# Seven block products in both stages of an AdaLN and low-rank FFN kernel

## The chip, the cores and the metric

The kernel runs on one core of one Trainium2 chip. The metric is the device time of one execution in microseconds, the median of several runs. PE is the matrix engine (TensorE), PEld its weight loads, ACT ScalarE, DVE VectorE, POOL GpSimd and SP the engine that issues the DMAs. Each engine takes its instructions in order and waits on semaphores.

## The reference, cut to what matters

`x` is 16 batches of 512 tokens by 1024 channels. Everything is float32.

```python
q_emb = relu(cond @ W3 + b3)                        # (16, 1024)
y = relu(((n * x + sum_over_tokens(x)) * q_emb[:, None, :]) @ W2 + b2)   # n = 512
base = y @ W_base + b_base                          # 1024 x 1024
shared = (y @ A_s) @ B_s                            # rank 16
gates = softmax(y @ W_router + b_router)            # 6 experts, the top 2 are kept
routed = sum over e of ((y @ A_r[e]) * w[e]) @ B_r[e]   # rank 16 each
out = x + base + shared + routed
```

The three factors `W_router`, `A_r` and `A_s` stand side by side in `acat` (1024 x 118), the `B` factors in `bcat` (118 x 1024).

## The kernel before

Activations lie transposed, channels on the 128 partitions and the 512 tokens of a batch along the free axis, so that a tile is 128 x 512. Every float32 product is three matmuls (`three`, L856 to L860): operands are split into a rounded high part (fp32r, made by ACT) and the low remainder (made by DVE, or by POOL for weights), and hi x hi, hi x lo and lo x hi are added up in PSUM.

**First stage** (W2), unrolled over eight pairs of batches. The 2 x 2 blocks are the two halves of the channels and the two batches of a pair: G11, G21 are batch 0, G12, G22 batch 1. Seven products of blocks replace eight (`NPROD`), in `product` (L902): four groups j of output tiles, each with four k, 16 threes in all. ACT loads and sums the x tiles (`source`, L495), waits for POOL's `shift_of` (L416), scales them, and makes the high parts (`high`, L516). DVE makes the low parts (`low`, L663) and the block sums (`t1` to `t4`). Partial results go from PSUM to the buffers `pbuf` and `ubuf` and are added there (`copy_p0`, `make_w`, `make_u`, L527 and L689); two sets of four banks alternate (`SETB`). Results go through `yring` and are stored in DRAM without the relu. Between these, SP and POOL split W_base into high and low, one 128 x 512 chunk at a time, two per pair (`load_wbase`, `save_wbase`, `split`).

**Second stage** (W_base), a loop of one batch (`batch`, L942) on each engine. y is loaded again (`load_y`), relu and the splits are made (`y_high`, `y_low`), and each of eight output tiles takes eight threes with W_base: 64 threes per batch. Beside them stand the eight threes of the projection on `acat` into bank 6, four small transposes of the router's rows (L959), the gate work on DVE (`gate`, L800, eleven small steps each waiting for the one before), four transposes of the gates (L967), the product with the gates, and eight threes of the low-rank factors (`low_rank`). `evac_out` (L789) adds bias and residual, and SP stores.

The order of work on each engine is written out by hand; nothing else plans it. SP holds all DMAs in one order, and a wait in it holds back all that follow. ACT's order in a pair, with the calls put on fewer lines:

```python
def pair(i, last=False):          # ACT, L549
    high(i, 1); source(i, G12); copy_p0(i)
    high(i, 2); source(i, G22); c11(i)
    high(i, 3); high(i, 4); high(i, 5)
    ...                           # next_first, high(i, 6), next_rest
```

Of the kernel before, what the change touches and what calls it, by code (L numbers as in the profile page):

```python
# [5 lines left out]
F32 = mybir.dt.float32  # L6
# [5 lines left out]
P = 128  # L12
PAIR = 2
# [13 lines left out]
H = 4  # L27
G11, G22, G12, G21 = range(4)
HELD_IN = [G11, G21, G12, G12, G11, G22, G21]
SETB = [0, 0, 1, 0, 1, 0, 1]  # L30
CONTINUES = (1, 6)
BATCH_OF = {G11: 0, G21: 0, G12: 1, G22: 1}
HALF_OF = {G11: 0, G21: 1, G12: 0, G22: 1}
SOURCE_NO = {G11: 0, G21: 1, G12: 2, G22: 3}


def adaln_ffn(nc, xT, condT, w3, b3, w2, b2, wbase, bbase, acat, bcat, brouter, outT, E, R):
# [6 lines left out]
    NCH = wbase.shape[0]  # L44
    CW = wbase.shape[2]
    HALF = K // 2
    WARM = 8
    OPS = NPROD * H

    y_dram = nc.dram_tensor("y_scratch", (NB, K, P, T), F32, kind="Internal").ap()  # L50
    wbh_dram = nc.dram_tensor("wb_hi_scratch", (NCH, P, CW), F32, kind="Internal").ap()
    wbl_dram = nc.dram_tensor("wb_lo_scratch", (NCH, P, CW), F32, kind="Internal").ap()

    with ExitStack() as ctx:
# [41 lines left out]
        sb("early_pad2", [P, NPROD * H, T], F32, early)  # L96
        sb("early_pad3", [P, 4 * H, T], F32, early)
# [5 lines left out]
        phase1 = ExitStack()  # L103
        w2_hi = sb("w2_hi", [P, NPROD, H, T], F32R, phase1)
        w2_lo = sb("w2_lo", [P, NPROD, H, T], F32R, phase1)
        phase1.close()

        wb_hi = sb("wb_hi", [P, 2, K, CW], F32R)  # L110
        a_hi = sb("a_hi", [P, K, AC], F32R)
        a_lo = sb("a_lo", [P, K, AC], F32R)
        sb("pad4", [P, H * T - 2 * K * AC])
        a_sb = sb("a_sb", [AC, T])
        hw = sb("hw", [AC, T])
        hw_hi = sb("hw_hi", [AC, T], F32R)
        hw_lo = sb("hw_lo", [AC, T], F32R)
        sb("pad5", [P, 4, T])
        wb_lo = sb("wb_lo", [P, 2, K, CW], F32R)
        low_hi = sb("low_hi", [AC, D], F32R)  # L120
        low_lo = sb("low_lo", [AC, D], F32R)
        wtok = sb("wtok", [P, TT, E])
        logits = sb("logits", [P, TT, E])
        lmax = sb("lmax", [P, TT])
        shifted = sb("shifted", [P, TT, E])
        ex = sb("ex", [P, TT, E])
        den = sb("den", [P, TT])
        rden = sb("rden", [P, TT])
        gates = sb("gates", [P, TT, E])
        beats = sb("beats", [P, TT, E, E])  # L130
        ties = sb("ties", [P, TT, E, E])
        rank = sb("rank", [P, TT, E])

        STAGE_AT = [H * G11 + k for k in range(H)] + [H * G22 + k for k in range(H)]
        RES_AT = [H * G12 + k for k in range(H)] + [H * G21 + k for k in range(H)]
# [3 lines left out]
        A_BANK, GATE_BANK = 6, 7  # L139
        Q_BANK, QT_BANK = 4, 6  # L140
        q_tok = [ps[:, QT_BANK + h, 0:HALF * NB].rearrange("p (m b) -> p m b", b=NB) for h in range(2)]
        tok = ps[:, GATE_BANK, 0:TT * E].rearrange("p (t c) -> p t c", t=TT)
# [71 lines left out]
        def slot(i, n, k):  # L214
            return H * ((i + n) % 2) + k
# [809 lines left out]
```

## Time and profile before

| | us |
|---|---|
| Median of 3 runs | 1557.67 (1557.47 to 1558.39) |
| Profiled execution | 1559.65 |
| Its span | 1557.8 |
| First stage, first matmul to last | 18.1 to 653.9 |
| Second stage | 658.1 to 1554.5 |
| PE / DVE / ACT / POOL busy | 1524.4 / 627.9 / 458.5 / 101.6 |

Matmuls are pipelined: a matmul lasts about 0.39 us, but the next one starts 0.23 us after it, so rows of single matmuls have to be read by their starts. A group's "idle before" counts only what remains after this overlap. Times in the rows are microseconds from the start of the span.

### The profile page before, as it was taken

The numbers are of one execution on the slowest core, as the hardware profiler recorded it, in microseconds if no ns is written. First come the engines' busy times: TensorE is split into PE (matmuls) and PEld (weight loads), VectorE is DVE, ScalarE is ACT, GpSimd is POOL, SyncE is SP. The second block draws the span as 40 slices with busy tenths as digits, with TensorE's granted clock in tenths as the row PEclk, the third lists the DMA queues.
The fourth block names the chain that finished last, engine by engine and source line by source line (L and its number), as shares of the span: only waits on it lengthen the run. The fifth ranks groups of instructions, "written<-read, shape, count | busy, mean of one in ns | idle before, by whom it ended". The sixth has DMA issues, their size and how long they took to land.

```text
span 1557.8 us, 18539 instructions
## 1 busy us (share of the span) xinstructions
PE 1524.4 (98%) x6688; PEld 1239.5 (80%) x6688; DVE 627.9 (40%) x1064; ACT 458.5 (29%) x869; POOL 101.6 (7%) x117
## 2 busy tenths in 40 slices
PE   6889999999999999899999999999999999999999
PEld 3668888888888888788888888888888888888887
DVE  3676555555646465612322321331232232233122
ACT  5646465555556564101101110110110110111010
POOL 2841000000000001000000000000000000000000
PEclk8899999999999999999999999999999999999999
DMA  7043425243434257434233323413413432341321
GB/s 277 28 155 116 165 105 169 98 160 108 149 108 166 92 179 275 161 112 162 75 117 131 119 83 121 162 40 121 162 65 114 145 107 95 121 161 41 121 108 54
DMA packets 107781, 196.67 MB, mean 126 GB/s; under 512 B 12258, under 2 KB 12258, under 8 KB 107736
## 3 DMA queue, kind: packets, MB, share of 16 engines
q1 hardware_dynamic: 107736, 196.10, 35.7%
q8 instruction: 25, 0.41, 0.1%
q14 instruction: 20, 0.16, 0.0%
HBM read 120.55 MB, written 75.50 MB: 126 GB/s over the span
## 4 chain that ended last, share of the span: by engine, by line
PE 95%; DVE 2%; ACT 1%; issue 1%; POOL 0%; DMA 0%; SPq 0%; DVEq 0%; POOLq 0%
PE ps L858 31%; PE ps L859 31%; PE ps L860 31%; DVE src L672 1%; DVE act_lo L667 1%; ACT src L505 0%; PE ps L967 0%; PE ps L959 0%; DMA src<-in_xT 0%; POOL w_lo L425 0%; ACT act_hi L524 0%; ACT w_hi L493 0%; DVE ubuf L693 0%; DVE w_lo L754 0%; ACT src L499 0%
## 5 line engine op out<-in xcount | busy, mean ns | idle before, releaser
L858 PE MATMUL ps<-act_hi,wb_hi 128*128 128x512 f32 x1024 | 404.1, 395 | 4.2 <-issue 4.2
L860 PE MATMUL ps<-act_hi,wb_lo 128*128 128x512 f32 x1024 | 400.5, 391 | 0.0
L859 PE MATMUL ps<-act_lo,wb_hi 128*128 128x512 f32 x1024 | 400.5, 391 | 0.0
L858 PE MATMUL ps<-act_hi,w_hi 128*128 128x512 f32 x896 | 351.0, 392 | 20.8 <-ACT pbuf L532 15.7
L859 PE MATMUL ps<-act_lo,w_hi 128*128 128x512 f32 x896 | 349.8, 390 | 0.0
L860 PE MATMUL ps<-act_hi,w_lo 128*128 128x512 f32 x896 | 349.8, 390 | 0.0
L858 PEld LDWEIGHTS ps<-act_hi,wb_hi 128*128 128x128 f32 x1024 | 192.7, 188 | 46.4 <-issue 4.6
L860 PEld LDWEIGHTS ps<-act_hi,wb_lo 128*128 128x128 f32 x1024 | 192.8, 188 | 41.9
L859 PEld LDWEIGHTS ps<-act_lo,wb_hi 128*128 128x128 f32 x1024 | 192.9, 188 | 40.4
L667 DVE TENSOR_TENSOR act_lo<-src,act_hi 128x512 fp32r<-128x512 f32 x224 | 158.6, 752 | 151.7 <-ACT act_hi L524 151.7
L858 PEld LDWEIGHTS ps<-act_hi,w_hi 128*128 128x128 f32 x896 | 169.1, 189 | 58.9 <-ACT pbuf L532 15.8
L859 PEld LDWEIGHTS ps<-act_lo,w_hi 128*128 128x128 f32 x896 | 169.2, 189 | 35.0
L860 PEld LDWEIGHTS ps<-act_hi,w_lo 128*128 128x128 f32 x896 | 168.9, 188 | 35.3
L524 ACT ACTIVATE act_hi<-src 128x512 fp32r<-128x512 f32 x220 | 132.4, 628 | 203.7 <-PE ps L860 187.9
L629 ACT ACTIVATE act_hi<-src 128x512 fp32r<-128x512 f32 x128 | 80.9, 632 | 237.4 <-PE ps L860 237.2
L811 DVE TENSOR_TENSOR logits<-ps,br_sb 128x24 f32<-128x24 f32 x16 | 2.9, 182 | 364.0 <-PE ps L959 364.0
L785 DVE SCALAR_TENSOR_TENSOR act_lo<-src,act_hi 128x512 fp32r<-128x512 f32 x128 | 88.4, 693 | 95.9 <-ACT act_hi L629 95.9
L795 DVE SCALAR_TENSOR_TENSOR src<-ps,bb_sb,src 128x512 f32<-128x512 f32 x128 | 87.6, 745 | 77.9 <-PE ps L860 77.9
L672 DVE TENSOR_TENSOR src<-src 128x512 f32<-128x512 f32 x128 | 91.1, 772 | 63.5 <-ACT src L505 63.5
L505 ACT ACTIVATE src<-src,shift,qn 128x512 f32<-128x512 f32 x124 | 91.0, 805 | 18.0 <-POOL shift L419 18.0
L633 ACT ACTIVATE a_sb<-ps 118x512 f32<-118x512 f32 x16 | 9.6, 597 | 283.8 <-PE ps L860 283.8
L499 ACT ACTIVATE src<-src 128x512 f32<-128x512 f32 x124 | 76.3, 617 | 16.7 <-DMA src<-in_xT 16.6
(84 smaller groups left out, 899.9 us busy)
## 6 DMA issues: line engine op xcount, KB each, us to landing
src<-in_xT SPq DMA_DIRECT2D x256, 256.0 KB, 3.9
y_scratch<-yring SPq DMA_DIRECT2D x128, 256.0 KB, 2.5
src<-y_scratch SPq DMA_DIRECT2D x128, 256.0 KB, 5.3
outT<-src SPq DMA_DIRECT2D x128, 256.0 KB, 2.1
r<-in_w SPq DMA_DIRECT2D x16, 256.0 KB, 7.8
wraw<-in_wbase SPq DMA_DIRECT2D x16, 256.0 KB, 3.3
wb_hi_scratch<-wst_hi SPq DMA_DIRECT2D x16, 256.0 KB, 2.0
wb_lo_scratch<-wst_lo SPq DMA_DIRECT2D x16, 256.0 KB, 2.5
```

What stands on the lines that cost most here:

```text
L499: nc.scalar.activation(src[:, t, :], src[:, t, :], ACT.Copy, accum_out=vsum[:, t:t + 1]).then_inc(x_summed, 1)
L505: nc.scalar.activation(src[:, t, :], src[:, t, :], ACT.Identity, bias=shift[:, t:t + 1], scale=qn[:, H * HALF_OF[g] + k, 2 * i + BATCH_OF[ ...
L524: nc.scalar.activation(act_hi[:, slot(i, n, k), :], src[:, H * HELD_IN[n] + k, :], ACT.Copy).then_inc(hi_done, 1)
L629: nc.scalar.activation(act_hi[:, k, :], src[:, STAGE_AT[k], :], ACT.Relu).then_inc(y_hi_done, 1)
L633: nc.scalar.activation(a_sb[:], ps[0:AC, A_BANK, :], ACT.Copy).then_inc(a_copied, 1)
L667: nc.vector.tensor_tensor(act_lo[:, s, :], src[:, H * HELD_IN[n] + k, :], act_hi[:, s, :].bitcast(F32), ALU.subtract).then_inc(lo_done, 1)
L672: nc.vector.tensor_tensor(src[:, H * out + k, :], src[:, H * a + k, :], src[:, H * b + k, :], ALU.subtract).then_inc(t_ready, 1)
L785: nc.vector.scalar_tensor_tensor(act_lo[:, k, :], src[:, STAGE_AT[k], :], 0.0, act_hi[:, k, :].bitcast(F32), ALU.max, ALU.subtract).then_i ...
L795: nc.vector.scalar_tensor_tensor(r, ps[:, bank, :], bb_sb[:, m:m + 1], r, ALU.add, ALU.add).then_inc(out_evac, 1)
L858: nc.tensor.matmul(out, w_hi, a_h, start=start, stop=False, skip_group_check=onto)
L859: nc.tensor.matmul(out, w_hi, a_l, start=False, stop=False, skip_group_check=onto)
L860: return nc.tensor.matmul(out, w_lo, a_h, start=False, stop=stop, skip_group_check=onto)
```

## The change

Both stages take pairs of batches and seven block products. The products 2, 3, 4 and 6 are added in PSUM onto what the banks hold (`ONTO`), so that banks 0 to 3 carry all the sums; product 1 goes to banks 4 and 5 and is added by DVE. Before a bank is accumulated further, ACT copies it (`copy_p0`, `copy_u2`, `copy_u4`) to `buf1` to `buf3`, in which the results are finished.

In the first stage the projections on `acat` (`project_y`, a `three` after a group of products 4, 5, 6 and of the next pair's 0), the transposes and the gate work are put between the products. For them y is split again (`y_high`, `y_low`); `y_low` writes over the buffer that was stored. The gated rows go to DRAM (`hw_dram`). The second stage only has the seven products, the low-rank threes and the residual; its low-rank input for product 6 is the difference of two batches.

W_base's seven block sums are made in the first stage in 60 pieces of at most 128 x 256 (`piece` on SP and on POOL), 4 in pair 0 and 10 or 9 in each of pairs 1 to 6, one set of buffers for all. Both stages are unrolled on all engines. The diff, cut to its core (`...` marks what is left out):

```diff
+ONTO = (2, 3, 4, 6)
+PIECES = [(k, c, n) for k in range(H) for c in range(2) for n in (3, 2, 4, 5, 0, 1, 6)]
+PIECES += [(None, c, None) for c in range(D // PW)]
...
+        @block.sync
+            def piece(step):
+                if step > 0:
...
+                    sp.wait_ge(prep_made, step)
...
+                        sp.dma_start(wbh_dram[n, :, k, cols], wh[:].bitcast(F32)).then_inc(prep_saved, 16)
+                        sp.dma_start(wbl_dram[n, :, k, cols], wl[:].bitcast(F32)).then_inc(prep_saved, 16)
+                    sp.wait_ge(prep_saved, 32 * step)
+                if step < len(PIECES):
...
+                    elif n == 3:
+                        raw(ws, Q21)
+                        raw(wt, Q22)
...
+            def pair(i):
+                todo = list(POINTS.get(i, range(0)))
...
+                point(9)
+                point(8)
...
+                for j in range(H):
+                    sp.wait_ge(relu_done, four(i, j))
+                    sp.dma_start(y_dram[2 * i, j], buf1[:, j, :]).then_inc(buf1_stored[j], 16)
+                point(7)
...
+                for k in range(H):
+                    sp.wait_ge(lo_done, op_no(i, 4, k))
+                    load_next(i, G22, k)
+                point(5)
...
+                point(4)
+                for k in range(H):
+                    sp.wait_ge(lo_done, op_no(i, 5, k))
+                    load_next(i, G11, k)
+                point(3)
+                if last:
+                    load_weights(4)
+                for j in range(H):
+                    sp.wait_ge(c12_done, four(i, j))
+                    sp.dma_start(y_dram[2 * i + 1, j], buf1[:, j, :]).then_inc(buf1_stored[j], 16)
+                point(2)
+                for k in range(H):
+                    sp.wait_ge(lo_done, op_no(i, 6, k))
+                    load_next(i, G21, k)
+                point(1)
+                if last:
+                    load_weights(5)
+                for j in range(H):
+                    sp.wait_ge(c22_done, four(i, j))
+                    sp.dma_start(y_dram[2 * i + 1, H + j], buf3[:, j, :]).then_inc(buf3_stored[j], 16)
+                point(0)
...
+        @block.gpsimd
+            for i in range(1, LAST):
+                todo = list(POINTS[i])
+                for q, more in ((G12, 6), (G22, 4), (G11, 2), (G21, 0)):
+                    while len(todo) > more:
+                        piece(todo.pop(0))
+                    shift_of(i + 1, q)
...
+        @block.scalar
+            def pair(i):
+                last = i == LAST
+                if i > 0:
+                    x_scale(i, G21)
+                    for j in range(H):
+                        high(i, 1, j)
+                        y_high(i - 1, C21, j)
+                        if j == 0:
+                            copy_h(i - 1, GB)
+                        else:
+                            copy_p0(i, j - 1)
+                    copy_p0(i, H - 1)
+                for j in range(H):
+                    high(i, 2, j)
+                    if j == 0 and i > 0:
+                        exponent(i - 1, GB)
+                    if j > 0:
+                        relu(i, j - 1)
...
+                for j in range(H):
+                    high(i, 4, j)
+                    if j > 0:
+                        copy_u4(i, j - 1)
+                    if j == 2 and i > 0:
+                        exponent(i - 1, GA)
+                    if j >= 2:
+                        y_high(i, C11, j - 2)
+                    if not last:
+                        x_sum(i + 1, G12, j)
+                copy_u4(i, H - 1)
+                if not last:
+                    x_scale(i + 1, G12)
+                for j in range(H):
+                    high(i, 5, j)
+                    if j > 0:
+                        c12(i, j - 1)
+                    if j in (1, 2):
+                        y_high(i, C11, j + 1)
+                    if not last:
+                        x_sum(i + 1, G22, j)
+                c12(i, H - 1)
+                if not last:
+                    x_scale(i + 1, G22)
+                for j in range(H):
+                    high(i, 6, j)
+                    y_high(i, C12, j)
+                    if not last:
+                        x_sum(i + 1, G11, j)
...
+        @block.vector
+            def y_low(i, c, j):
+                if c == C11:
+                    dve.wait_ge(buf1_stored[j], 16 * (2 * i + 1))
...
+            def pair(i):
+                if i > 0:
+                    c21(i - 1, H - 1)
+                    for j in range(H):
+                        low(i, 1, j)
+                        y_low(i - 1, C21, j)
+                        t2(i, j)
+                    gate_logits(i - 1, GB)
+                    gate_weights(i - 1, GB)
+                for j in range(H):
+                    low(i, 2, j)
+                    if j > 0:
+                        c11(i, j - 1)
...
+                for j in range(H):
+                    low(i, 4, j)
+                    if j == 1 and i > 0:
+                        gate_logits(i - 1, GA)
...
+                if i > 0:
+                    gate_weights(i - 1, GA)
...
+                for j in range(H):
+                    low(i, 6, j)
+                    if j > 0:
+                        c22(i, j - 1)
+                    y_low(i, C12, j)
...
+        @block.tensor
+            def pair(i):
+                for j in range(H):
+                    group(i, 0, j)
+                    if i > 0:
+                        project_y(i - 1, C21, j)
+                        if j == 1:
+                            turn_h(i - 1, GB)
+                    elif j == 0:
+                        turn(1)
...
+                for j in range(H):
+                    group(i, 1, j)
+                    if j == 2 and i > 0:
+                        turn_gates(i - 1, GB)
+                for j in range(H):
+                    group(i, 2, j)
+                if i > 0:
+                    turn_h(i - 1, GA)
+                for j in range(H):
+                    group(i, 3, j)
+                if i > 0:
+                    turn_gates(i - 1, GA)
+                for j in range(H):
+                    group(i, 4, j)
+                    project_y(i, C11, j)
+                for j in range(H):
+                    group(i, 5, j)
+                    project_y(i, C12, j)
+                for j in range(H):
+                    group(i, 6, j)
+                    project_y(i, C22, j)
```

In `group`, product 1 waits for `c11_done` of group j - 2 before it takes a Z bank again; `c12` on ACT waits for `project_y` to have read C11 from the same buffer; `y_high` uses two tiles in turn and waits for the `project_y` two before.

## Rows read from the trace of the kernel before

**Rows 1.** The page, parts 1 and 2: busy us; tenths of the granted clock in 40 slices.

```profile
PE 1524.4 (98%) x6688; PEld 1239.5 (80%) x6688; DVE 627.9 (40%) x1064; ACT 458.5 (29%) x869; POOL 101.6 (7%) x117
...
PEclk8899999999999999999999999999999999999999
```

**Rows 2.** The page, part 4: the chain that ended last, by engine.

```profile
PE 95%; DVE 2%; ACT 1%; issue 1%; POOL 0%; DMA 0%; SPq 0%; DVEq 0%; POOLq 0%
```

**Rows 3.** Groups by line, forms apart: first matmul of each three.

```profile
L858 PE MATMUL ps<-act_hi,wb_hi 128*128 128x512 f32 x1024 | 404.1, 395 | 4.2 <-issue 4.2
...
L858 PE MATMUL ps<-act_hi,w_hi 128*128 128x512 f32 x896 | 351.0, 392 | 20.8 <-ACT pbuf L532 15.7 <-issue 2.7 <-DVE act_lo L667 2.4
...
L858 PE MATMUL ps<-act_hi,a_hi 128*118 128x512 f32 x128 | 50.4, 394 | 0.0
...
L858 PE MATMUL ps<-hw_hi,low_hi 118*128 118x512 f32 x128 | 50.2, 392 | 0.0
```

**Rows 4.** One pair by windows; then PE timeline: gate transposes of batches 0, 1.

```profile
120.60:196.80 76.20, 76.20 (x338) 63.06 (x336) 44.06 (x70) 43.82 (x87) 4.50 (x8) 1.00 0.43 149
...
694.56 0.60 PE L967 MATMUL ps<-ident,wrow 128*118 128x128 f32 x4
...
750.39 0.60 PE L967 MATMUL ps<-ident,wrow 128*118 128x128 f32 x4
```

**Rows 5.** PE timeline: start, us, instruction, idle; the three long idle times.

```profile
29.28 0.42 PE L875 MATMUL ps<-ident,qrow 16*128 16x16 f32 x4
45.41 0.80 PE L858 MATMUL ps<-act_hi,w_hi 128*128 128x512 f32 x1 [15.71 <-ACT pbuf L532]
...
105.36 0.39 PE L860 MATMUL ps<-act_hi,w_lo 128*128 128x512 f32 x1
108.22 0.76 PE L858 MATMUL ps<-act_hi,w_hi 128*128 128x512 f32 x1 [2.47 <-issue]
...
653.53 0.39 PE L860 MATMUL ps<-act_hi,w_lo 128*128 128x512 f32 x1
658.11 0.77 PE L858 MATMUL ps<-act_hi,wb_hi 128*128 128x512 f32 x1 [4.19 <-issue]
```

**Rows 6.** PE timeline behind the second of them.

```profile
109.64 0.63 PE L858 MATMUL ps<-act_hi,w_hi 128*128 128x512 f32 x1
110.07 0.63 PE L859 MATMUL ps<-act_lo,w_hi 128*128 128x512 f32 x1
```

**Rows 7.** ACT and DVE timeline in pair 1: scales, a copy, splits.

```profile
213.32 2.94 ACT L505 ACTIVATE src<-src,shift,qn 128x512 f32<-128x512 f32 x4 [0.31 <-POOL shift L419]
...
218.76 0.69 ACT L539 ACTIVATE yring<-ps,b_sb 128x512 f32<-128x512 f32 x1 [0.79 <-PE ps L860]
219.34 2.19 ACT L524 ACTIVATE act_hi<-src 128x512 fp32r<-128x512 f32 x4
...
220.00 2.50 DVE L667 TENSOR_TENSOR act_lo<-src,act_hi 128x512 fp32r<-128x512 f32 x4 [1.22 <-ACT act_hi L524]
```

**Rows 8.** Timeline of one gate: exponent, and the last step.

```profile
741.49 0.22 ACT L635 ACTIVATE ex<-shifted 128x24 f32<-128x24 f32 x1 [7.19 <-DVE shifted L814]
...
744.31 0.36 DVE L833 COPY wrow<-wtok 128x384 f32<-128x384 f32 x1
```

**Rows 9.** SP timeline; page part 6; L267 and L282 after 575 us: landings.

```profile
588.56 0.44 SPq L271 DMA_DIRECT2D wraw<-in_wbase  x1
593.92 0.32 SPq L275 DMA_DIRECT2D wb_hi_scratch<-wst_hi  x1
...
wb_lo_scratch<-wst_lo SPq DMA_DIRECT2D x16, 256.0 KB, 2.5
...
DMA to landing us min/median/max: 2.0/2.1/8.8
...
DMA to landing us min/median/max: 5.8/8.5/12.5
```

**Rows 10.** DVE and POOL timeline in pair 0, both busy.

```profile
70.69 6.88 DVE L672 TENSOR_TENSOR src<-src 128x512 f32<-128x512 f32 x4
...
66.78 6.84 POOL L430 TENSOR_TENSOR r<-r,s 128x512 f32<-128x512 f32 x4
```

**Rows 11.** The last matmul; the span ends at 1557.8.

```profile
1554.13 0.39 PE L860 MATMUL ps<-hw_hi,low_lo 118*128 118x512 f32 x1
```

More of the change, by code:

```diff
@@ L28 @@
 G11, G22, G12, G21 = range(4)
[L29 to L31 removed]
+ONTO = (2, 3, 4, 6)
 BATCH_OF = {G11: 0, G21: 0, G12: 1, G22: 1}
 HALF_OF = {G11: 0, G21: 1, G12: 0, G22: 1}
[L34 removed]
+C11, C12, C22, C21 = range(4)
+GB, GA = range(2)
+Q11, Q12, Q21, Q22 = range(4)
 def adaln_ffn(nc, xT, condT, w3, b3, w2, b2, wbase, bbase, acat, bcat, brouter, outT, E, R):
@@ L125, in adaln_ffn @@
[L125 to L135, printed above, removed]
+        ha_hi = sb("ha_hi", [AC, T], F32R)
@@ new lines, in gate_no, with loads @@
+        def gate_no(i, w):
+            return 2 * i + w + 1
+        def loads(g, q, n=0):
+            if g < NP:
+                return 16 * (g + 1)
+            return 16 * (NP + {G11: 1, G21: 1, G12: 3, G22: 2}[q] * (g - NP) + n + 1)
+        tile = lambda q, k: H * q + k
+        STEPS = 11
+        PIECES = [(k, c, n) for k in range(H) for c in range(2) for n in (3, 2, 4, 5, 0, 1, 6)]
+        PIECES += [(None, c, None) for c in range(D // PW)]
+        PIECE_LOADS = [2 if n in (3, 5) else 1 for _, _, n in PIECES]
@@ new lines, in high @@
+            def high(g, n, k, first=False):
+                func, source = ACT.Copy, src
+                if n == 2:
+                    source, t = buf3, k
+                else:
+                    t = tile({0: G11, 1: G21, 3: G12, 4: G22, 5: G11, 6: G21}[n], k)
+                if n == 2:
+                    act.wait_ge(t2_made, four(g, k))
+                elif n == 3:
+                    act.wait_ge(t1_made, four(g, k))
+                elif n == 5:
+                    act.wait_ge(t3_made, four(g, k))
+                elif n == 6:
+                    act.wait_ge(t4_made, four(g, k))
+                elif g < NP:
+                    act.wait_ge(x1_ready, tile_no(g, {0: G11, 1: G21, 4: G22}[n], k))
+                else:
+                    act.wait_ge(x_loaded[t], loads(g, {0: G11, 1: G21, 4: G22}[n]))
+                    func = ACT.Copy if n == 0 else ACT.Relu
+                if not first:
+                    free(g, n, k)
+                nc.scalar.activation(act_hi[:, slot(g, n, k), :], source[:, t, :], func).then_inc(hi_done, 1)
@@ L645, in _ @@
+            for p in range(NP):
+                pair2(p)
         @block.vector
```

1500 lines of the change are left out of this document (900 added, 600 removed).

## The prediction, made before the changed kernel ran

> **What bounds the kernel now.** I read the busy shares first: PE 98% at full granted clock except in the first two slices [rows 1]. The chain that ended last is PE for 95% of the span, under the three lines of `three` [rows 2]. So the time is a count of matmuls, one after the other, plus what PE loses between them. The count is in the groups by line [rows 3]: 1024 + 896 + 128 + 128 = 2176 threes, 6528 matmuls. Their 390 ns is latency; the price of one is its distance from the next. One pair of the first stage is 7 x 16 x 3 = 336 matmuls in 76.20 us without a gap [rows 4], 0.2268 us each. One batch of the second is 750.39 - 694.56 = 55.83 us [rows 4]; its 240 matmuls are 54.43, so its eight transposes cost 1.40.
>
> What PE loses: 16.1 us before the second product of pair 0, 2.9 before its last, 4.6 between the stages [rows 5]. After each of them the matmuls stand 0.43 us apart for a while, at the lower of the two clocks [rows 5, 6]: 1.5 us lost behind the 2.5 us of idle, 2.2 behind the 15.7, 2.3 behind the 4.2. With 3.5 for late `act_lo` in pair 0 the start loses 26.1 in all (pair 1 begins near 120.6; 18.14 + 76.2 would be 94.4) and the switch of stages 6.7. Check: 18.14 + 6528 x 0.2268 + 16 x 1.40 + 26.1 + 6.7 + 3.7 for the tail = 1557.6, against a span of 1557.8 (execution 1559.65).
>
> **What the change removes from PE.** The W_base stage goes from 8 x 8 to 7 x 8 blocks for a pair's 4 quadrants: 384 tile products per pair of batches become 336, so 3072 matmuls become 2688. Projections (384), low-rank products (384) and transposes keep their number and move. 384 x 0.2268 = **-87.1 us**. The stage switch disappears in its old form: y comes in while the last pair runs. **-6.7**, +0.5 for the gate work of the last pair.
>
> Everything else is queue order. I carried the order of ACT, DVE, POOL and SP through one pair, with the distances of the rows: ACT split 0.54 (2.19 for 4), scale 0.73 (2.94 for 4), DVE split 0.62, one PSUM copy 0.6 [rows 7], a three-matmul group of four 12 x 0.2268 = 2.72, and a `project_y` 0.68. A new pair is 384 matmuls and two sets of transposes, 89.9 us, if nothing waits.
>
> **Gates.** `gate_weights` for GB follows `exponent`, which is behind `copy_p0(3)`, so after product 0. It takes 744.67 - 741.49 = 3.2 us [rows 8]; `low` 0 and 1 and `c11(0)` follow it on DVE, and product 1's third group waits for `c11(0)` in its Z bank: end of product 0, +0.9 (copy, split), +3.2, +1.2, +0.7 = 6.0 against 5.4: 0.45 late. For GA, `gate_weights` waits behind `low(4,3)`, whose split waits on ACT behind `copy_u4(1)`, thus for half of product 3. From there to the weights I count 6.3 us, and PE has 5.4: 0.9 late at `turn_gates(GA)`. Together 1.35 x 7 pairs = **+9.5** (bounds 0 and 20: DVE and ACT are busy for 44 of 76 us [rows 4]).
>
> **ACT order at products 4 and 5.** This is the wait I am surest of. `c12(3)` needs the end of product 4 with its last `project_y`. Behind it ACT has `x_scale(i+1,G22)` (2.94), then `high(6,0)` (0.54), then `y_high(C12,0)`; DVE then makes `y_low(C12,0)`. End of product 4 + 0.2 + 0.6 + 2.94 + 0.54 + 0.65 + 0.7 = 5.7 us. PE asks for it after one group, 2.72. It stands 3.0 to 3.1 us, in-order, with everything of product 5 behind it. Pairs 1 to 6: **+18.6** (pair 0 is in the start). Bounds 0, if the order were otherwise released, and 6 x 4.5.
>
> **Weight pieces.** 60 pieces of 128 x 256 go through one set of buffers. One cycle is SP's two stores and their landing, one or two loads and their landing, then POOL. The old kernel's nearest row, of 256 KB: load issued at 588.56, store issued at 593.92, 5.4 us; a store lands in 2.5 [rows 9]. With half of the bytes and half of POOL's elements I take 4.4 + 0.1 + 2.9 = 7.4 us per piece (bounds 6.5 and 8.3). Nine or ten pieces per pair fit in 90 us, but the last six are in a row, and SP holds the C22 stores, POOL the shifts of G11 and G21, behind them. With the C12 wait above, P1 is done about when C22's stores are due: 6 x 7.4 - 2.7 + 1 = 42.7 us after the start of product 4, where 41.7 is early enough. Some 0.5 to 1 us late. Also POOL's operations now meet DVE's: in the old pair 0 a DVE subtraction stood 1.7 us from the next while POOL ran, 0.62 otherwise [rows 7, 10]. A piece's operations are half as long, so a meeting costs up to 0.65. I take 1.0 for both, 6 pairs: **+6** (0 to 30).
>
> The Trainium skill (DMA: Bandwidth & Descriptors, Anatomy of one DMA) gives a DMA about 2.0 us fixed plus bytes over 436 GB/s, 2.3 us for 128 KB; a cycle would be 6.6 us by it (an estimate from that page) and the term for the pieces near 0. The row shows 2.5 us for a 256 KB store, where the page has 2.6. The skill (SBUF — State Buffer, Who interferes with whom) calls the port shared by DVE and GpSimd an exclusive lock for a whole instruction; 1.7 us against 0.62 agrees, and by it `c11` and the other PSUM reads are spared.
>
> **Last pair of the first stage.** Here SP issues 2 MB of weights when product 4 ends and again when product 5 ends, ahead of the stores of C12 and C22. `y_low` overwrites the stored buffer, so it waits for the landing. Stores behind such a load took up to 8.8 us, others 2.0; the 1 MB loads themselves land after 5.8 to 12.5 [rows 9]. I take a landing 7.6 after the product's start, near the row behind a load, plus 0.8 for the split, against 2.72: 5.7 late, twice, **+11.4** (0 to 15).
>
> **Start.** q is turned after the first group, so product 1 starts near 29.5, not 45.4. But its third group waits for `c11(0)`, and that is behind copy_p0, behind both scales: about 46.8, with a slow clock after it. Product 3 waits for `low(3,3)` under POOL's lock, near 69. Product 4 starts near 80, the C12 wait comes, and P2 can't be made before the shift of G11, 25 us after product 4's start; so C22's stores go out 38 us after it and PE stands 7.9 at `project_y(C22,0)`. Pair 1 begins near 131.8; 18.1 + 372 x 0.2268 would be 102.5. Loss 29.3 against 26.1: **+3.2** (-8 to +12).
>
> **Clock.** The waits of 3 us and more each look like those that lowered the clock [rows 5, 6]. Ten of them (six at C12, two in pair 0, two in pair 7) at 1.0 (1.5 to 2.3 in the rows, 0 behind waits of 0.7): **+10** (0 to 20).
>
> **Second stage.** By the same bookkeeping nothing is late: 28 splits, 12 copies and 3 small splits are 24 us of ACT in 87; Z banks have 2 us to spare, residual loads about 4. 0 (0 to 8 in all; 2 us of spare per pair are no proof). Unrolling changes nothing for PE: the first stage was unrolled and gapless [rows 4], the loop loses nothing that the groups show. The tail keeps its 3.7 [rows 11].
>
> **Sum.** -87.1 - 6.7 + 0.5 + 9.5 + 18.6 + 6 + 11.4 + 3.2 + 10 = -34.6. On the profiled execution's 1559.65 that is 1525; the median of the runs stands 2.0 below it (1557.67), so **1523 us**, with its own range 1508 to 1545.
>
> **Rivals.** *Order only*: the C12 wait and the gates stay, but stores, pieces and clock hide (a store that lands in 2.0, a cycle under 7). -87.1 - 6.2 + 3.2 + 9.5 + 18.6 = -62: **1496**. For it: my DMA prices are medians of a busier queue. Against it: idles of 2.5 us did lower the clock.
> *All hidden*: PE stays gapless as it was from 121 to 653. -87.1 - 6.7 + 3: **1467**. Against it: the C12 wait is in the order of the instructions; for it to vanish, x_scale would have to be off ACT's path. If the products removed are not 384, the matmul count shows it, and the forecast fails as a whole.
> *Slower*: SP and POOL set the pair. Its place is the row of six pieces at products 4 to 6. Each 0.1 us on the cycle costs 0.6 per pair. From 8.4 us per piece the 33 us that are left of the gain (six pairs, 5.6 each) are gone; at 8.8 the time is near **1573**. For it: the loads have 1 KB runs and there are two of them in some pieces; the 256 KB row is at 5.4 + 2.9 = 8.3. Against it: half of the bytes, half of the elements.
>
> **Chances.** Forecast 0.48, order only 0.23, all hidden 0.13, slower 0.12, and 0.04 near no change. 0.2% is 3 us, about what a measurement can tell. Faster 0.85, same 0.03, slower 0.12. The range 1478 to 1558 leaves out about 0.2: most of all hidden and of slower.
>
> **What would show it.** Matmul groups must be 896 + 896 threes of w. PE's idle before `project_y`'s first line should name DVE `y_low` (buf1_lo) about 3 us, six or seven times, and ACT's queue just before should be four scales. Idle before the transposes of wrow near 0.9. In the last pair `buf1_lo` and `buf3_lo` should wait for y_scratch stores. In the last 700 us PE should be gapless, 87.1 per pair. If pairs 1 to 6 are 90 us apart, the whole queue argument is wrong; if they are over 103, the pieces rule. Expected: 96 to 98.

## The result, and the profile after

| | before | after |
|---|---|---|
| Median | 1558.03 us (4 runs, 1557.47 to 1559.3) | 1616.54 us (4 runs, 1616.12 to 1620.28) |
| Ratio, 95% interval | | 1.038 (1.0362 to 1.0398) |
| Span, profiled execution | 1557.8 | 1614.6 |
| PE matmul instructions | 6688 | 6304 |

The change makes the kernel 58.5 us slower. The forecast was 1523.

The page of the changed kernel: busy shares (part 1), the granted clock, the chain by engine [rows 1, 2].
```profile
PE 1499.2 (93%) x6304; PEld 1183.3 (73%) x6304; DVE 893.3 (55%) x1488; ACT 663.3 (41%) x1273; POOL 163.0 (10%) x231
...
PEclk9899999999999999998999899999999999999999
...
PE 46%; DMA 5%; DVE 1%; SPq 0%; issue 0%; ACT 0%; POOLq 0%; POOL 0%; ACTq 0%; DVEq 0%
```
384 matmuls are gone as forecast, yet PE is idle for 7% where it was for 2%, and DMA transfers stand in the chain.

Pairs by windows: start and end, length, then PE, PEld, DVE, ACT, POOL busy (instructions), granted clock, DMA share, GB/s. The lines are pairs 1, 5, 6, 7 of the first stage (pairs count from 0), pairs 0 and 3 of the second [rows 4 has the pair of before, 76.20].
```profile
134.93:237.67 102.74, 96.06 (x402) 75.79 (x401) 55.82 (x101) 58.44 (x116) 17.93 (x28) 0.95 0.38 128
537.02:637.65 100.63, 95.30 (x402) 74.92 (x401) 55.62 (x101) 56.12 (x113) 17.73 (x28) 0.97 0.38 128
637.65:754.07 116.42, 95.33 (x402) 74.76 (x401) 55.98 (x101) 56.20 (x114) 14.51 (x24) 0.93 0.33 107
754.07:872.51 118.44, 98.31 (x402) 77.22 (x401) 52.96 (x101) 41.09 (x74) 0.12 (x1) 0.91 0.51 184
872.51:984.77 112.26, 99.33 (x414) 77.30 (x413) 59.69 (x112) 27.93 (x51) 0.00 (x0) 0.94 0.44 151
1163.70:1253.17 89.47, 89.47 (x386) 72.21 (x385) 51.17 (x80) 24.66 (x43) 0.00 (x0) 1.00 0.44 149
```
Two things were not forecast. Pairs 1 to 5 take 99.6 to 102.7 instead of 96 to 98, and pair 6, pair 7 and the first pair of the second stage 112 to 118. And a pair of 384 matmuls without any gap takes 89.47 and not 87.1: its matmuls stand 0.233 us apart, not 0.2268. I call this distance, from the start of one matmul to the start of the next, the pitch.

What PE waited for (releaser, us in total, times, longest):
```profile
PE ps L1307 <- DVE buf_lo L1037: 32.6, 8, 6.9
PE ps L1307 <- DVE buf_lo L1039: 27.3, 6, 11.5
PE ps L1406 <- ACT a_sb L751: 15.9, 7, 4.5
PE ps L1307 <- DVE buf L1002: 12.1, 3, 11.0
PE ps L1307 <- DMA low_lo<-low_lo_scratch: 8.4, 1, 8.4
...
PE ps L1412 <- DVE wrow L1082: 4.0, 6, 1.1
```
L1037 is `y_low` of C11 and C12 (all eight waits at C12), L1039 that of C22 and C21, L751 `copy_h`, L1002 the additions (`c11` in pair 0). Lines 1, 2 and 6 are waits of the forecast, in its places, save for the 13.5 us of line 2 that fall in pair 6; lines 3 and 5 are new. Where I give single waits below, I take them from start to start of the matmuls, less one pitch; the view's idle time is 0.16 us less, since it counts from the end of the matmul before.

**First new cause: transfers of 118 rows.** In the first lines below, windows of the changed kernel, SP has just issued the two stores of low-rank rows (743 to 747) and the loads of `low_hi`, `low_lo` and `ha_raw` (892 to 902).
```profile
743.00:747.00 4.00, 4.00 (x15) 3.17 (x15) 2.27 (x5) 1.77 (x4) 0.00 (x0) 0.79 0.13 43
...
892.00:902.00 10.00, 7.41 (x36) 5.38 (x34) 1.78 (x3) 0.00 (x0) 0.00 (x0) 0.98 0.13 53
```
The share of DMA time is 0.13, as two engines out of 16 would show, at 43 and 53 GB/s. With 120 rows (experiment e3) the same loads show:
```profile
847.00:849.00 2.00, 2.00 (x10) 1.60 (x9) 1.76 (x8) 0.91 (x2) 0.00 (x0) 1.00 0.89 248
```
118 is 2 x 59. The Trainium skill (DMA: Bandwidth & Descriptors, Why a DMA increments its semaphore by 16 and not by 1) says that a DMA runs on the largest number of engines up to 16 that divides the slowest dimension of both its sides, which gives 2 for 118 and 15 for 120 (my estimate from it). The shares of 0.13 and 0.89 agree.

The kernel before has one such transfer, the 118-row load of `bcat` (472 KB), and its trace could have warned:
```profile
658.41 0.36 SPq L365 DMA_DIRECT2D wraw<-in_bcat  x1
...
672.97 1.04 POOL L481 CAST low_hi<-wraw 118x1024 fp32r<-118x1024 f32 x1 [37.11 <-DMA wraw<-in_bcat]
```
POOL gets it 14.6 us after its issue; the 1 MB loads of 128 rows landed after 5.8 to 12.5 [rows 9]. Nothing on PE's path waited for it there.

Who waits for such a transfer is seen in the changed kernel's timeline. This is what touches `a_sb` around the transposes of GA in pair 1:
```profile
166.17 0.33 SPq L384 DMA_DIRECT2D hw_scratch<-a_sb  x1
...
173.55 0.60 ACT L751 ACTIVATE a_sb<-ps 118x512 f32<-118x512 f32 x1 [6.02 <-DMA hw_scratch<-a_sb]
...
174.20 0.41 PE L1406 MATMUL ps<-ident,a_sb 6*128 6x6 f32 x4 [1.71 <-ACT a_sb L751]
```
`copy_h` of GA writes the buffer from which the rows of GB are being stored, so it waits for that store, 7.4 us after its issue, and PE behind it. In pair 6 the last weight pieces have 118 rows (SP timeline):
```profile
713.63 0.25 SPq L349 DMA_DIRECT2D low_hi_scratch<-wh  x1
713.92 0.38 SPq L350 DMA_DIRECT2D low_lo_scratch<-wl  x1
720.67 0.24 SPq L363 DMA_DIRECT2D ws<-in_bcat  x1
720.95 1.31 SPq L314 DMA_DIRECT2D src<-in_xT  x3
```
SP stood 6.4 us for two stores to land (until their data had arrived), with the stores and loads of the pair behind it; the longest wait at C22, 11.5 us, is at 741.35 in this pair.

### The profile page after: what moved, and what is told of

It reads as the page before. It is cut to its first block, busy times and chain, and to the rows that moved or that the text cites. A ratio compares the mean times of both kernels' runs of the same rounds, so it can differ in the third digit from the quotient of the medians.

```text
span 1614.6 us, 18512 instructions
## 1 busy us (share of the span) xinstructions
PE 1499.2 (93%) x6304; PEld 1183.3 (73%) x6304; DVE 893.3 (55%) x1488; ACT 663.3 (41%) x1273; POOL 163.0 (10%) x231
## 4 chain that ended last, share of the span: by engine, by line
PE 46%; DMA 5%; DVE 1%; SPq 0%; issue 0%; ACT 0%; POOLq 0%; POOL 0%; ACTq 0%; DVEq 0%
PE ps L1307 16%; PE ps L1309 15%; PE ps L1308 15%; DMA ha_raw<-hw_scratch 2%; DMA y_scratch<-buf 1%; DMA hw_scratch<-a_sb 1%; DMA outT<-buf 1%; DMA hb_raw<-hw_scratch 0%; DMA low_lo_scratch<-wl 0%; DMA ws<-in_bcat 0%; DVE buf L1002 0%; DMA buf<-in_xT 0%; SPq L519 0%; DVE act_lo L957 0%; ACT act_hi L690 0%
## 5 line engine op out<-in xcount | busy, mean ns | idle before, releaser
L1307 PE MATMUL ps<-act_hi,w_hi 128*128 128x512 f32 x1792 | 723.7, 404 | 25.0 <-DVE buf L1002 12.1
L1308 PE MATMUL ps<-act_lo,w_hi 128*128 128x512 f32 x1792 | 716.9, 400 | 0.0
L1309 PE MATMUL ps<-act_hi,w_lo 128*128 128x512 f32 x1792 | 716.8, 400 | 0.0
L1307 PEld LDWEIGHTS ps<-act_hi,w_hi 128*128 128x128 f32 x1792 | 343.3, 192 | 113.4 <-DVE buf L1002 15.6
L1309 PEld LDWEIGHTS ps<-act_hi,w_lo 128*128 128x128 f32 x1792 | 342.4, 191 | 83.0
L1308 PEld LDWEIGHTS ps<-act_lo,w_hi 128*128 128x128 f32 x1792 | 343.6, 192 | 80.8
L1002 DVE SCALAR_TENSOR_TENSOR buf<-ps,bb_sb,buf 128x512 f32<-128x512 f32 x128 | 95.7, 749 | 155.4 <-PE ps L1309 142.8
L1002 DVE SCALAR_TENSOR_TENSOR buf<-ps,b_sb,buf 128x512 f32<-128x512 f32 x96 | 71.7, 747 | 83.2 <-PE ps L1309 83.1
L709 ACT ACTIVATE yhi<-buf 128x512 fp32r<-128x512 f32 x128 | 80.0, 625 | 88.7 <-PE ps L1309 88.7
L717 ACT ACTIVATE buf<-ps 128x512 f32<-128x512 f32 x64 | 37.9, 597 | 129.3 <-PE ps L1309 129.3
L725 ACT ACTIVATE buf<-ps 128x512 f32<-128x512 f32 x64 | 37.4, 597 | 105.4 <-PE ps L1309 105.4
L733 ACT ACTIVATE buf<-ps 128x512 f32<-128x512 f32 x64 | 38.3, 598 | 87.6 <-PE ps L1309 87.6
L1039 DVE SCALAR_TENSOR_TENSOR buf_lo<-buf,yhi 128x512 fp32r<-128x512 f32 x64 | 48.0, 750 | 29.9 <-DMA y_scratch<-buf 29.9
L1037 DVE TENSOR_TENSOR buf_lo<-buf,yhi 128x512 fp32r<-128x512 f32 x64 | 47.5, 752 | 28.3 <-ACT yhi L709 17.2
```

The costliest lines, as they stand in the source:

```text
L709: nc.scalar.activation(yhi[:, (y_no(i, c, j) - 1) % 2, :], buf[:, j, :], func).then_inc(yhi_done, 1)
L1002: nc.vector.scalar_tensor_tensor(buf, ps[:, bank, :], bias, buf, ALU.add, ALU.add).then_inc(done, 1)
L1037: nc.vector.tensor_tensor(lo, y, hi, ALU.subtract).then_inc(ylo_done, 1)
L1039: nc.vector.scalar_tensor_tensor(lo, y, 0.0, hi, ALU.max, ALU.subtract).then_inc(ylo_done, 1)
L1307: nc.tensor.matmul(out, wh, a_h, start=start, stop=False, skip_group_check=onto)
L1308: nc.tensor.matmul(out, wh, a_l, start=False, stop=False, skip_group_check=onto)
```

## The experiments

Each run names its edit against the changed kernel unless it says otherwise. The kernel before had medians of 1558.4 to 1558.8 beside them.

**e1, e2: where the weights begin in SBUF.** The tiles' start addresses in both kernels gave the idea: `act_hi` and `act_lo` begin 128 bytes past a multiple of 512 in both, the weights 128 past before and 160 past after, since the 32-byte `bb_sb` now stands ahead of `w_hi`.
```diff
         bb_sb = sb("bb_sb", [P, K])
+        sb("align_pad", [P, K])          # e1; e2: the kernel before, a pad behind wrow
```


> The changed kernel with one unused tile of 32 bytes behind bb_sb, so that w_hi and w_lo begin at multiples of 64 bytes in SBUF, as w2_hi and w2_lo did in the kernel before; nothing else differs. Theory A (the start address of the weights sets the pitch: every product of the changed kernel has a matmul each 233.2 ns, all of the kernel before 226.7): the pitch goes to 226.7, the time from 1616 to 1576 (6.5 ns x 6144 = 40), between 1570 and 1582, and the waits stay. Rival B (the pitch belongs to what else changed, partial sums that go on in a filled bank, the other engines' traffic, unrolled code): no change, 1614 to 1619, pitch 233.

> The kernel before with one unused tile of 32 bytes behind wrow, so that all its weights (w2, wb, low and others) begin 32 bytes past a multiple of 64. Theory A: pitch 226.7 -> 233.2 in both stages, 6528 matmuls x 6.5 ns = +42 us, 1600 (1592 to 1604). Rival B: unchanged, 1556 to 1560.

Measured: e1 1623.14 (ratio 1.0413, 1.0396 to 1.0431), pitch as in the changed kernel, so theory A as I had put it is wrong. e2 1588.84 (ratio 1.0194, 1.0177 to 1.0211): the kernel before loses 30 us by an unused tile of 32 bytes. Its pair 1, against 76.20 in [rows 4]:
```profile
120.12:198.52 78.40, 78.40 (x338) 63.13 (x336) 44.14 (x70) 43.61 (x86) 4.49 (x8) 1.00 0.42 144
```
336 matmuls at 0.2333. I had expected 42 us for 6528 matmuls and not 30: in this run the products of W_base go from 0.2280 on average to 0.2331, which is less than 6.5 ns, and the 768 matmuls on `a_hi`, `a_lo` and the low-rank weights hardly change (0.6 ns and 0 on average). The address matters, but what about it?

**e5: a multiple of 128** (pad of 96 bytes). **e9: 128 past a multiple of 512** (`bb_sb` behind `w_lo`). **e10: the kernel before, 32 bytes ahead of `act_hi`**, so that everything is shifted together. **e14: 256 apart** (pad of 224 bytes; e10 and e14 have one run each).

> The changed kernel with 96 unused bytes behind bb_sb: w_hi, w_lo and the low-rank weights begin at multiples of 128 bytes (in the changed kernel 32 past one, with the first 32-byte tile 64 past one, in the kernel before 0). Theory A (a matmul's pitch is 226.7 ns where its weights begin at a multiple of 128 bytes and 233 where not): pitch 226.7 in all products, 1616 -> 1576 (1570 to 1582), waits unchanged. Rival B (the kernel before has its pitch for another reason, and the 32 bytes moved another of its tiles too): pitch 233, 1612 to 1624.

> The changed kernel with bb_sb declared behind w_lo and not ahead of w_hi, so that w_hi and w_lo begin 128 bytes past a multiple of 512, as act_hi and act_lo do and as w2_hi and w2_lo did in the kernel before (offsets 160, 192 and 256 gave 233.1, 233.1 and 232.4 ns). The low-rank weights stay at offset 160. Theory C (the pitch is 226.7 only where weights and moving data have one offset in 512, or where the weights' is 128): the 42 x 8 products of a pair go to 226.7, low-rank products not, 1616 -> 1578 (1570 to 1584). Rival B (address is one condition, a second comes with the change itself, in the code or in the traffic of the other engines): 232 or more, 1611 to 1622.

> The kernel before with 32 unused bytes ahead of act_hi, so that act_hi, act_lo and all weights begin at offset 160 in 512: the weights as in the shifted kernel of 1588.84, but now with the moving data at the same offset. Theory C1 (only the difference between the two counts): pitch 226.7, time 1557 to 1560. Theory C2 (the absolute address of the weights counts): pitch 233.5 and 1586 to 1592, or more.

> The changed kernel with 224 unused bytes behind bb_sb: weights at offset 384 in 512 bytes, moving data at 128, so 256 apart. If equality in 256 is enough: pitch 226.7 and 87.4 to 87.8 us per pair in the second stage. If it must be in 512 (or 256 apart is no better than 32, 64 and 128 apart): 232 to 233.5 and 89.3 to 89.8.

A pair of the second stage in e5, e9 and e14, then pair 1 of e10, by windows:
```profile
1162.30:1251.65 89.35, 89.35 (x386) 72.39 (x385) 51.29 (x80) 24.64 (x43) 0.00 (x0) 1.00 0.45 150
```
```profile
1162.20:1249.99 87.79, 87.79 (x386) 72.24 (x385) 51.30 (x80) 24.64 (x43) 0.00 (x0) 1.00 0.45 152
```
```profile
1162.20:1249.83 87.63, 87.63 (x385) 72.25 (x385) 51.28 (x80) 24.64 (x43) 0.00 (x0) 1.00 0.44 153
```
```profile
118.68:194.84 76.16, 76.16 (x338) 63.06 (x337) 44.09 (x70) 44.28 (x88) 4.49 (x8) 1.00 0.44 152
```
| start of the weights minus start of the moving data, bytes in 512 | pitch inside a row of products on w, us |
|---|---|
| 0 (before, first stage; e9; e10, both shifted) | 0.2266 |
| 32 (after; e2) | 0.233 |
| 64 (e1) | 0.233 |
| 128 (e5) | 0.2325 |
| 256 (e14) | 0.2266 |

So neither the address of the weights nor its alignment counts, but the difference to the moving operand: e10 has the weights where e2 has them, and runs in 1557.30. Differences of 0 and 256 are alike, which fits a rule within 256 bytes; more values were not tried. The table is of rows of products on w alone. The low-rank threes don't follow it: those of GA, whose own weights and moving data begin alike in e9 and in e13, stand 0.233 to 0.238 apart in e9, and in e13, where everything begins alike, still 0.2326 and 0.2359. A change from one kind of offset to another costs too: in e9 the three matmuls behind each low-rank three stand 0.2355, 0.2317 and 0.2291 apart. So a pair is 87.79 in e9, and 87.36 where all start addresses agree (e12, e13).

The time did not follow the pitch. e9 takes 1606.39 (expected 1578; ratio 1.031, 1.0293 to 1.0328), e5 1614.26, e14 1605.99. In e9 the second stage gives back 12 us (7 x 1.68 and a little in its first pair), the first stage nothing: from the start of pair 1 to that of pair 7 it takes 622 us, the changed kernel 619. A faster PE only waits longer there; something else sets the pairs.

**e3, e6: rows.**
```diff
-    AC = E + (E + 1) * R
+    AC = 2 + E + (E + 1) * R             # and zeros in acat and bcat; e6: 4 +
```


> The changed kernel with two zero columns added to A and two zero rows to B, so that the low-rank rows, the stores and loads of hw_scratch, bcat and low_hi / low_lo have 120 rows and not 118. Theory A (a transfer of 118 = 2 x 59 rows runs on few of the 16 DMA engines; 120 = 15 x 8 on 15): a store of hw_scratch lands in about 2.5 us and not 6.75, PE's waits before the transposes of h (1.7 to 2.3 in a pair, 15.9 in all) go, the C22 wait of pair 6 falls from 11.5 to under 7, and the wait for low_lo (8.4) goes: 1616 -> 1586 (1576 to 1594). Rival B (the transfers are late because they queue behind others, not for their shape): within 4 us of 1616.

> The changed kernel with 122 low-rank rows (four of zeros) and not 118 or 120. 122 is 2 x 61. Theory A (the number of DMA engines of a transfer is the largest divisor up to 16 of its rows: 2 for 118, 15 for 120, 2 for 122): all of the slowness of the 118-row kernel is back, stores of hw_scratch land in 6.5 to 7 us, the time is 1610 to 1620. Rival B (only 120 or more rows, or a multiple of 8 or of 2, matters): near 1554, landing under 3.5.

Measured: e3 1554.04 (ratio 0.9971, 0.9959 to 0.9982), 62.5 us below the changed kernel where I expected 30; e6 1629.34 (one run, expected 1610 to 1620). In e6 the loads of `low_hi`, `low_lo` and `ha_raw` show:
```profile
902.00:906.00 4.00, 4.00 (x19) 3.04 (x18) 3.45 (x6) 0.00 (x0) 0.00 (x0) 1.00 0.13 53
```
More rows, an even number as before, and slow again at the same share: so it is neither the number of rows nor their evenness. Eight engines could show 0.5 at most, where e3 has 0.89. The divisor of the rule fits all three; other row counts were not tried. Pairs 1, 6, 7 and the first of the second stage in e3:
```profile
135.00:233.40 98.40, 94.62 (x401) 74.87 (x400) 56.07 (x101) 58.66 (x118) 18.20 (x28) 0.97 0.41 134
...
623.40:721.50 98.10, 94.86 (x401) 74.78 (x400) 56.06 (x101) 59.98 (x120) 15.38 (x24) 0.97 0.39 128
721.50:831.40 109.90, 95.36 (x402) 75.27 (x402) 53.01 (x101) 37.38 (x69) 0.00 (x0) 0.94 0.56 198
831.40:925.60 94.20, 94.20 (x414) 75.63 (x413) 59.73 (x112) 28.02 (x51) 0.00 (x0) 1.00 0.55 180
```
18.3 us come back in pair 6, 8.5 in pair 7, 18.1 in the first pair of the second stage, some 14 in pairs 1 to 5 together. I had counted only the waits that name such a transfer. The rest I put down to the stores and loads queued behind one and to the slow clock after each wait; no run separates these two.

**e13: both causes away, nothing else.**
```diff
+    AC = 2 + E + (E + 1) * R
...                                      # zeros in acat and bcat as in e3
-        bb_sb = sb("bb_sb", [P, K])
...
         w_lo = sb("w_lo", [P, NPROD, H, T], F32R)
+        bb_sb = sb("bb_sb", [P, K])
+        sb("align_pad", [P, P - K])
```


> The changed kernel with 120 low-rank rows, and with its weights at the offset in 512 bytes of the moving data (bb_sb and 480 unused bytes behind w_lo), and nothing else. Theory A (the two are the forecast's whole error): the 120-row kernel's 1554, less 8 x 2.0 in the second stage, less 1.4 in each pair of the first that PE paces and 0 where the pieces do: 1528 to 1538. Rival B (the offset is hidden in the first stage and partly covers other waits there): 1538 to 1545. If the forecast's terms were wrong and only added up, pairs 1 to 6 are not 96 to 98 apart.

Measured: 1529.24 (ratio 0.9819, 0.9802 to 0.9837). This is the change as the forecast had priced it, and it stands 6 us above 1523. Pairs 1 and 5, and 7 (each window begins 1.4 us before the pair's first matmul and is as long as the pair):
```profile
133.30:229.10 95.80, 91.97 (x402) 73.93 (x401) 55.69 (x100) 59.81 (x119) 18.29 (x28) 0.98 0.41 137
519.00:615.20 96.20, 92.28 (x402) 73.94 (x401) 56.99 (x100) 55.03 (x112) 19.50 (x28) 0.98 0.40 134
...
710.00:818.60 108.60, 94.80 (x401) 75.76 (x401) 52.96 (x100) 37.78 (x70) 0.00 (x0) 0.94 0.56 201
```

**e4: the scales on ACT.** Instead of `x_scale(i + 1, G22)` ahead of product 6's loop:
```diff
                 for j in range(H):
                     high(i, 6, j)
                     y_high(i, C12, j)
+                    x_scale(i + 1, G22, (j,))
```


> The changed kernel with ACT's four scales of the next pair's G22 put one behind each y_high of C12, and not all four between c12(3) and high(6,0). Theory A (the prediction's: PE's wait before project_y of C12 is the order of ACT): the 2.8 to 3.8 us before buf1_lo in pairs 0 to 5 fall below 0.6, with 1 to 1.5 us of slow clock behind each: 1616 -> 1588 (1582 to 1600), less if y_low of C22 or the first product of the next pair is late in its place. Rival B (DVE or the shift of POOL holds y_low, not ACT): the wait stays within 0.5 us and so does the time, 1612 to 1618.

Measured: 1621.39 (ratio 1.039, 1.037 to 1.0411; expected 1588), nothing gained. The wait at C12 is gone in pair 0 and is 3.4 to 4.3 us in pairs 1 to 5, where the changed kernel has 3.2 to 4.0. In the changed kernel, around 204 us, ACT had:
```profile
203.42 0.69 ACT L743 ACTIVATE buf<-ps,b_sb 128x512 f32<-128x512 f32 x1 [2.18 <-PE ps L1309]
204.01 2.92 ACT L658 ACTIVATE src<-src,shift,qn 128x512 f32<-128x512 f32 x4
206.83 0.62 ACT L690 ACTIVATE act_hi<-src 128x512 fp32r<-128x512 f32 x1
207.35 0.62 ACT L709 ACTIVATE yhi<-buf 128x512 fp32r<-128x512 f32 x1
...
209.08 0.70 DVE L1037 TENSOR_TENSOR buf_lo<-buf,yhi 128x512 fp32r<-128x512 f32 x1 [0.90 <-DMA y_scratch<-buf]
209.92 0.75 PE L1307 MATMUL ps<-yhi,a_hi 128*118 128x512 f32 x1 [3.83 <-DVE buf_lo L1037]
```
That is the queue of the forecast, step by step, but DVE's last 0.9 us are for the store of C12. In e4 all of the wait is the store's:
```profile
202.85 1.87 SPq L454 DMA_DIRECT2D y_scratch<-buf  x4
...
205.37 0.69 DVE L1036 TENSOR_TENSOR buf_lo<-buf,yhi 128x512 fp32r<-128x512 f32 x1 [3.24 <-DMA y_scratch<-buf]
```
SP issues it behind a weight piece whose stores it lets land first. Two causes end within a microsecond of each other; the view names the last one alone.

**e7: both holds of C12 away** (in e3: the scales spread, SP's four stores of C12 issued ahead of `point(3)`). **e11: e7, and SP doesn't wait for a piece's stores to land. e15: e3 with that alone.**
```diff
-                    sp.wait_ge(prep_saved, 32 * step)
+                    if step == len(PIECES):
+                        sp.wait_ge(prep_saved, 32 * step)
```


> The 120-row kernel with both holds of y_low(C12) taken away: ACT's four scales of G22 spread behind the y_high of C12, and SP's four stores of C12 issued ahead of a weight piece and not behind it. Theory A (the C12 wait has two causes that end within a microsecond of each other, the scales on ACT and the store on SP, so that removing one moved nothing): the waits of 3.0 to 4.0 us before buf1_lo in pairs 1 to 6 go below 0.8, and the slow clock behind them: 1554 -> 1524 (1516 to 1532). Rival B (a third cause, y_used or POOL's lock on DVE, stands at the same place): 1548 to 1556.

> The kernel e7 (120 rows, scales spread, C12 stored ahead of a piece) in which SP no longer waits for a piece's two stores to land before it goes on; POOL waits for them anyway before it writes wh again. Theory A (in e7 the six pieces in a row at products 4 to 6, 6.2 to 9 us each, hold SP's stores and POOL's shifts, and the waits of 4 to 6 us at C22 are theirs): a cycle falls by about 2 us, the C22 waits below 1, with 2 us of slow clock behind each: 1567 -> 1524 (1518 to 1538). Rival B (the C22 wait is the shift of G11 and the scales behind it on ACT, with POOL's work between them, not SP): waits stay over 3 us, 1555 to 1568.

> The 120-row kernel in which SP doesn't wait for the landing of a piece's stores, with ACT's four scales and the store of C12 where the change has them. Against e11 (1533), which differs by those two alone. Theory A (the scales cost what the forecast said as soon as nothing else holds that place): C12 waits of 2.9 to 3.1 in pairs 1 to 6 and up to 1.5 of slow clock behind each, the C22 waits of 1.6 gone: 1533 + 6 x 2 to 2.7 + 3 for pair 0 = 1548 to 1553. Rival B (a wait at C12 or one at C22, whichever, costs the same): 1530 to 1538.

e7: 1567.59 (ratio 1.0052, 1.0035 to 1.0069; expected 1524), 13.5 slower than e3. The C12 waits are gone before the last pair, but for 1.7 us in pair 5, and one of 4 to 6 us stands at C22 in each of pairs 1 to 6: SP takes up the piece behind the C12 stores later, and all that follow it, so that it issues the C22 stores at 216.97, behind a store landing.
```profile
216.97 1.87 SPq L464 DMA_DIRECT2D y_scratch<-buf  x4
...
219.42 1.09 DVE L1038 SCALAR_TENSOR_TENSOR buf_lo<-buf,yhi 128x512 fp32r<-128x512 f32 x1 [1.31 <-DMA y_scratch<-buf]
```
e11: 1533.41 (ratio 0.9844, 0.9828 to 0.9861), 34 us below e7; so SP's wait for each piece's stores was the hold. e15: 1549.64 (ratio 0.9949, 0.9932 to 0.9965), 4.4 below e3, less than its own runs differ (1542.09 to 1552.5). PE's waits at C12 (L1038) and C22 (L1040) in e15:
```profile
PE ps L1308 <- DVE buf_lo L1038: 26.7, 8, 6.9
PE ps L1308 <- DVE buf_lo L1040: 11.8, 2, 6.7
```
Every C12 wait of pairs 0 to 6 in it is 2.98 us (3.05 in pair 1), which is the order on ACT and nothing else: DVE begins `buf_lo` as soon as it has done its `act_lo`, and waits for no store. e15 to e11 is 16 us by the medians and 11 by the two profiled executions, of which e15's is the fastest of its four: the price of this order, less the waits of 0.9 to 1.9 us at C22 that take its place in pairs 1 to 5 of e11. (e11 also issues the C12 stores earlier; in e15 nothing waits for them.)

**e8, e12: mended kernels.** e8 is e7 with the 96 bytes, `load_weights(4)` and `(5)` behind the stores of C12 and C22, and no pieces in pair 0. e12 is e8 with equal offsets everywhere (in place of the 96 bytes) and the edit of e11.
```diff
                     sp.dma_start(y_dram[2 * i + 1, j], buf1[:, j, :]).then_inc(buf1_stored[j], 16)
+                if last:
+                    load_weights(4)
...                                      # load_weights(5) likewise
+        POINTS = {0: range(0, 0)}
```


> The kernel of the run before with three more: the 96 bytes, the weights of W_base for products 4 and 5 loaded behind the stores of C12 and C22 in the last pair, and no weight pieces in pair 0 (ten in each of pairs 1 to 6). If the account of the changed kernel's time holds: 1524 - 40 for the pitch - 7 for C22 in pair 0 - 14 and 3 of clock for the last pair = 1460, between 1455 and 1480, well below the kernel before. If the waits only move to the pieces or the gates: 1485 to 1510.

> The mended kernel e8 (1535) with bb_sb behind w_lo and 480 bytes behind it in place of the 96, which puts the low-rank weights too at 128 past 512, and without SP's wait for the landing of a piece's stores. Theories C and A together: 1535 - 41 - 36 = 1458 (1448 to 1470). C alone 1494, A alone 1499, neither 1535.

Measured: e8 1535.05 (ratio 0.9838, 0.9821 to 0.9856; expected 1455 to 1480): neither of its two premises held. The pitch stayed at 0.2325, and the C22 waits were those of e7. Pair 7, which has no pieces, went from 109.5 in e7 to 92.2. e12: **1477.48** (ratio 0.9485, 0.9469 to 0.9501), 5% faster than before and 139 us below the changed kernel, but 19 above what I expected: 1.5 to 2.2 us at C22 remain in pairs 1, 2, 4 and 5. Its pair 3 and pair 7:
```profile
307.30:398.40 91.10, 90.42 (x401) 72.78 (x401) 58.24 (x100) 56.47 (x115) 20.83 (x30) 1.00 0.45 146
...
675.70:766.80 91.10, 90.43 (x402) 72.82 (x401) 52.89 (x100) 37.44 (x69) 0.00 (x0) 1.00 0.65 239
```

## Why the prediction was wrong

By its own terms, each against the run that shows it best (e13 is the changed kernel without the two causes below):

| term | forecast | measured |
|---|---|---|
| 384 matmuls | -87.1 | gone; a gapless pair is 87.36 at equal offsets (e13), 89.47 in the changed kernel |
| stage switch | -6.7 + 0.5 | no gap at the switch in e13 |
| gates | +9.5 | 4.6 before the transposes of `wrow` (e13), 0.4 before those of h |
| C12, order on ACT | 3.1 x 6 = +18.6 | 2.98 x 6 (e15); 19.7 in e13 |
| pieces, POOL's lock | +6 | 1.7 at C22 and C21 in e13; 4.4 from e3 to e15, of the size of the scatter |
| last pair, two loads | 5.7 x 2 = +11.4 | 6.84 + 7.01 (e13); 17 with the clock (e7 to e8) |
| start | pair 1 at 131.8, +3.2 | 134.8 (e13), which is +6.2 in the same sum; 134.93 (after) |
| slow clock | +10 | 13.4 behind the start in e13 (70 matmuls 0.35 to 0.5 us apart, each less 0.227) |
| second stage | 0 | gapless in e13, save for the pitch |
| transfers of 118 rows | none | +62.5 (e3) |
| offset of the weights | none | +24.8 (e3 to e13); 10.2 alone (e9) |

1616.5 - 62.5 - 24.8 = 1529.2, the forecast 6 us off. The two causes don't simply add up: with the 118 rows still there, the offset gives back 10 us (e9), and 25 once they are gone.

The step that failed first is the price of a transfer, taken from its bytes alone. It stands in "With half of the bytes and half of POOL's elements I take 4.4 + 0.1 + 2.9 = 7.4 us per piece", in the 0 for the second stage, and in the stores of the gated rows, which have no term at all. For the 56 pieces of 128 rows 7.4 was fair: in e3 SP's loads for four pieces in a row stand at 185.39, 192.37, 199.56 and 206.98, 7.0 to 7.4 apart. The four of 118 rows took 13.6 to 13.8 (loads at 706.88 and 720.67). A store of `hw_scratch` took 7.4 on the path to GA's transposes; with 120 rows it lands in 2.8 (median of the 15 in e3's trace). The first pair of the second stage got 18.1 us shorter with 120 rows. The formula that the prediction quotes from the Trainium skill (DMA: Bandwidth & Descriptors, Anatomy of one DMA) is given there for DMAs issued from GpSimd, while here SP issues them; by it such a store takes 2.6 us (an estimate from that page), which agrees with the 2.8 and not with the 7.4.

The second step that failed is the pitch: 0.2268 was taken over from [rows 4] as a property of the instruction, though those rows show it for one layout of SBUF only.

That e13 comes within 6 us is in part luck. Gates, C12, pieces, last pair, start and clock are 58.7 us together in the forecast and 59.9 in e13 (5.0, 19.7, 1.7, 13.9, 6.2, 13.4), but gates and pieces were 9 too dear, and the start, the last pair and the clock 9 too cheap. In the gates the sum was off too: 6.0 against 5.4 is 0.6 late and not 0.45.

The rival *slower* was right about the sign and named the right engines, SP and POOL holding stores behind six pieces. Its condition, a cycle above 8.4 us, was met by the 118-row pieces alone, and its mark, over 103 us per pair, was not met in pairs 1 to 5 (99.6 to 102.7). e9 shows that there too PE was not the pace, and e7 that what is taken from C12 comes back at C22. *Order only* is refuted: pieces, stores and clock all cost. The forecast's mark for the C12 wait, four scales in ACT's queue, was met and would have misled: e4 shows that a second cause stood behind it.

What stays open: why the difference of the start addresses matters to PE, why the low-rank threes stand 0.2326 to 0.2359 apart even where it is 0 (e13), why e6 is 13 us slower than the changed kernel (one run), and how the slow clock falls on one wait of 2.98 and not on the next: in e15 two of six such waits in pairs 1 to 6 cost 1.3 us more, four nothing.

## What to carry to other kernels

Before pricing a DMA look at its row count, not only its bytes, and factor it: 118 rows cost 62 us here, two rows of zeros gave them back. When a wait is found, look for the second cause behind it before pricing its removal: SP's store and ACT's scales released DVE within 0.9 us of each other, and taking one away moved nothing. And when tiles are moved in SBUF, measure the pitch of a gapless stretch again.

## What the runs showed of the hardware

- A 128x512 fp32r matmul with a weight load each followed the one before by 0.2266 us where the start addresses of weights and moving operand in SBUF differed by 0 or 256 bytes (modulo 512; before, e9, e10, e14), by 0.2325 to 0.2335 where they differed by 32, 64 or 128 (after, e1, e2, e5). This is of rows of products on w, whose strides inside both tiles are multiples of 512 bytes; the low-rank threes of 118 and 120 rows don't follow it. The 32-byte shift alone cost the kernel before 30 us of 1558.6.
- Loads and stores of 118 rows show a DMA share of 0.13 at 43 to 53 GB/s, loads of 122 rows 0.13 at 53, of 120 rows 0.89 at 248 GB/s.
